# Sums of squares for the head norms: ScalarE's accumulator output in place of a VectorE reduction

## What is computed

```python
def _ln(x, w, b):
    mu = jnp.mean(x, axis=-1, keepdims=True)
    var = jnp.mean(jnp.square(x - mu), axis=-1, keepdims=True)
    return (x - mu) * jax.lax.rsqrt(var + EPS) * w + b

q = _fp8_linear_pertensor(ln_out, wq, wq_scale, q_in_scale).reshape(b, s, g, hpg, d)
q = _ln(q, qln_w, qln_b)
k = _fp8_linear_pertensor(ln_out, wk, wk_scale, k_in_scale).reshape(b, s, g, d)
k = _ln(k, kln_w, kln_b)
v = _fp8_linear_pertensor(ln_out, wv, wv_scale, v_in_scale).reshape(b, s, g, d)
core = _gqa(q, k, v).reshape(b, s, nh * d)
```

## Time and profile before

| | before |
|---|---|
| median of 3 runs | 2023.72 us (2023.13 to 2024.34) |
| profiled execution, its own time | 2026.58 us |
| its span in the trace | 2024.8 us |
| busy PE / DVE / ACT / POOL | 85% / 76% / 70% / 58% |
| granted clock of TensorE, mean | 0.977 |
| DMA | 240.88 MB, mean 119 GB/s |

### The profile page before, as it was taken

How to read it: one execution, slowest core, us unless ns; L and a number is a source line. 1 busy time by engine, 2 the same in 40 slices (tenths; PEclk the granted TensorE clock), 3 DMA queues, 4 the chain that set the end, 5 groups by cost and what they waited for, 6 DMA issues and landing times.

```text
span 2024.8 us, 48234 instructions
## 1 busy us (share of the span) xinstructions
PE 1722.7 (85%) x15776; PEld 1235.7 (61%) x15776; DVE 1531.0 (76%) x3480; ACT 1408.5 (70%) x2926; POOL 1172.4 (58%) x1045
## 2 busy tenths in 40 slices
PE   0015989999998999998999999999999768999998
PEld 0014767876776777677777767776877433444443
DVE  8996799899789979988997998899878633233232
ACT  2235889988988888898888889888999724030211
POOL 3454667776776777777777777677777602120202
PEclk9997999999999999999999999999999878999999
DMA  4100576776687677767767766776789983021100
GB/s 143 49 31 1 100 137 122 141 140 133 120 143 138 120 131 141 134 125 138 142 114 133 144 124 132 141 142 112 143 162 169 226 255 142 11 115 52 72 21 21
DMA packets 639383, 240.88 MB, mean 119 GB/s; under 512 B 612496, under 2 KB 612496, under 8 KB 638608
## 3 DMA queue, kind: packets, MB, share of 16 engines
q1 hardware_dynamic: 639120, 237.62, 57.8%
HBM read 65.57 MB, written 20.97 MB: 43 GB/s over the span
## 4 chain that ended last, share of the span: by engine, by line
issue 44%; POOL 32%; DVE 8%; ACT 6%; PE 6%; SPq 1%; DMA 1%; POOLq 1%; DVEq 0%; ACTq 0%
POOL local L976 16%; POOL head_rstd L952 7%; POOL local L959 6%; POOL local L990 3%; PE ps_pj L564 2%; ACT local L765 1%; ACT local L839 1%; DVE local L1093 1%; ACT local L842 1%; SPq L458 1%; DMA local<-local 1%; DVE local L1089 1%; DVE local L1069 1%; DVE local L1080 1%; ACT local L786 1%
## 5 line engine op out<-in xcount | busy, mean ns | idle before, releaser
L976 POOL TENSOR_TENSOR local<-local 128x512 bf16<-128x512 f32 x512 | 602.2, 1176 | 396.7 <-ACT local L842 396.7
L564 PE MATMUL ps_pj<-wide 128*128 (+2 forms) x5544 | 589.9, 256 | 10.2 <-ACT local L765 8.2
L564 PEld LDWEIGHTS ps_pj<-wide 128*128 128x128 bf16 x5544 | 471.2, 99 | 130.3 <-issue 11.5
L839 ACT ACTIVATE local<-ps_s,neg_max 128x512 f32<-128x512 f32 x512 | 375.8, 734 | 117.9 <-DVE neg_max L1191 117.0
L614 PE MATMUL ps_o<-v_hi,local 128*128 128x129 bf16 x2048 | 382.9, 224 | 71.9 <-DMA local<-local 31.5
L842 ACT ACTIVATE local<-ps_s,neg_max 128x512 bf16<-128x512 f32 x512 | 376.7, 736 | 13.6 <-DMA local<-local 13.6
L1191 DVE TENSOR_REDUCE neg_max<-ps_s 128x1 f32<-128x512 f32 x512 | 345.3, 674 | 54.0 <-PE ps_s L630 53.4
L616 PE MATMUL ps_o<-v_hi,local 128*128 128x129 bf16 x2048 | 381.9, 221 | 0.0
L615 PE MATMUL ps_o<-local 128*128 128x128 bf16 x2048 | 381.7, 220 | 0.0
L614 PEld LDWEIGHTS ps_o<-v_hi,local 128*128 128x128 bf16 x2048 | 200.9, 98 | 101.9 <-DVE local L1199 43.6
L765 ACT ACTIVATE local<-ps_pj,head_rstd 128x128 f32<-128x128 f32 x756 | 231.1, 407 | 36.9 <-POOL head_rstd L952 36.4
(11 more groups left out here) (111 smaller groups left out, 2866.9 us busy)
## 6 DMA issues: line engine op xcount, KB each, us to landing
w_raw<-w_group SPq DMA_DIRECT2D x32, 512.0 KB, 3.9
quantised_heads<-local SPq DMA_DIRECT2D x32, 512.0 KB, 3.4
wide<-quantised_heads SPq DMA_DIRECT2D x4, 4096.0 KB, 14.0
local<-local SPq DMA_TRANSPOSE x640, 3.2
local<-x SPq DMA_DIRECT2D x4, 1024.0 KB, 5.8
local<-ctx_t SPq DMA_DIRECT2D x4, 1024.0 KB, 5.0
w_raw<-w_proj SPq DMA_DIRECT2D x8, 512.0 KB, 4.5
wide<-w_proj SPq DMA_DIRECT2D x4, 1024.0 KB, 6.1
```

The lines of the kernel that those rows point to most:

```text
L564: last = mm(dst[:, at:at + n], lhs, w_at(par, part, c, cross * 512 + at, n), start=(k == 0), stop=(k == len(terms) - 1))
L839: a(p_exp[:, u % 2], ps_s[u % 2][:], ACT.Exp, bias=neg_max[:, u % 4:u % 4 + 1])
L976: tt_(pp[:, u % PP_BUFS, 1], p_exp[:, u % 2], pp[:, u % PP_BUFS, 0], ALU.subtract)\
```

## The change

ACT's one square over 384 columns becomes three over 128, one for each head, each with an accumulator output into that head's column of `sq_sum`. DVE's `head_squares` and the semaphore `red_done` go. `sq` gets two buffers and bf16 for F32; nothing reads it. The squares of tile t wait from t = 2 on for `var_done` to reach t - 1, in place of `red_done` reaching t. DVE's first instruction of a tile is now `v_rest`, and `head_variance` waits for `sq_done`.

```diff
-        sq = carve([3 * D], F32)
+        sq = carve([2, 3 * D], BF16)
...
             def squares(i, t):
                 act.wait_ge(proj_done, t + 1)
-                act.wait_ge(red_done, t)
-                a(sq[:], tile_bank(i, t)[:, 0:3 * D], ACT.Square).then_inc(sq_done, 1)
+                if not isinstance(t, int) or t >= 2:
+                    act.wait_ge(var_done, t - 1)
+                for h in range(3):
+                    last = a(sq[:, i % 2, h * D:(h + 1) * D], tile_bank(i, t)[:, h * D:(h + 1) * D], ACT.Square,
+                             accum_out=sq_sum[:, i % 2, h:h + 1])
+                last.then_inc(sq_done, 1)
...
-            def head_squares(i, t):
-
+            def head_variance(i, t):
                 dve.wait_ge(sq_done, t + 1)
-                v.tensor_reduce(sq_sum[:, i % 2, 0:3], sq[:].rearrange("p (h d) -> p h d", h=3), AX_X, ALU.add)\
-                    .then_inc(red_done, 1)
-
-            def head_variance(i, t):
-                dve.wait_ge(red_done, t + 1)
                 v.tensor_scalar(head_var[:, i % 2, 0:3], sq_sum[:, i % 2, 0:3], 1.0 / D, EPS, ALU.mult, ALU.add)\
                     .then_inc(var_done, 1)
...
             for i in range(TILES):
-                head_squares(i, i)
                 v_rest(0, i, i)
                 head_variance(i, i)
...
                     for k in tile_at(slot, VAR_LAG, first, last):
-                        head_squares(tile_place(k)[1], GROUP_TILES * g + TILES + k)
                         v_rest(*tile_place(k), GROUP_TILES * g + TILES + k)
                         head_variance(tile_place(k)[1], GROUP_TILES * g + TILES + k)
```

More of the change, by code:

```diff
@@ L241, in block_kernel @@
         vlo_done = sem("vlo_done")
-        red_done = sem("red_done")
         var_done = sem("var_done")
```

## The result

The changed kernel takes 2033.3 us (median of 5, 2032.1 to 2036.7) against 2023.3 for the kernel before in the same comparison: ratio 1.0054, 95% interval 1.0039 to 1.0068. It is slower by 10 us. I had forecast slower, but by 41 us.

A forecast was written before the change was run, and what follows sets the result against it. PE, DVE and ACT, close together and waiting for each other, bound the kernel; ACT would become fullest. +5.4 us a pass over 7.9 passes, +42.6, less 1.5 at the start, gave +41: 2065 us, range 1996 to 2140.

The forecast's parts named there:

- the first rival: Whole kernel: accumulator nearly free, a head at 0.16 to 0.25 us, so faster, about 2003 us; chance 0.28.
- I take 0.35: ScalarE's squares: each head's square with accumulator costs 0.35 us, so a tile grows by 0.68 us.
- the sum over a pass: Loop pass: ACT's load becomes 177.1 us, so a pass takes 180.9 to 187.9, middle 184.4 against 179.
- 7.9 passes: Loop with first and last pass: 252 squares at 32 a pass; +5.4 us a pass gives +42.6 us.
- 7 x 0.47 = 3.3 us a pass: PE's 7 waits for DVE in a pass: each 0.47 us shorter without the sum, about 3.3 us gained.
- The third rival: Whole kernel: DVE's gain and ACT's loss cancel, a head near 0.30 us, within 0.2% of 2024 us; chance 0.10.

The follow-up runs named there:

- the cost alone: Three ScalarE squares with accumulator outputs into a tile nobody reads, VectorE's sum and old wait kept, against the kernel before: 2072.8 us against 2026.0, ratio 1.0231.

## Why the prediction was wrong

**Right:** DVE's new wait behind v_part (20.1 us, above 7.5) and the fall of both waits for DVE (15.2 to 3.9 and 6.0 to 1.9). ACT did become the fullest engine of a pass, but only just: 166.78 us against PE's 166.30 and DVE's 148.16. Of VectorE the Trainium skill states that an operation which also writes out its accumulator is two instructions ("VectorE: DVE Perf Modes", section "Two Vector instructions with no wait between them"). For ScalarE the trace shows the same: it names the read, x756. The start gained 1.9 us, as forecast (1.5), though not through the new wait.

**The direction was luck.** I forecast a pass of the loop 5.4 us longer, and it became 0.3 longer. The changed kernel is slower because of its last pass, whose stretches I had not looked at. Of my signs, ACT's busy time went up by 11.5 us a pass where I wanted 15 or more, and PE's wait for ACT at ps_s fell from 3.2 to 2.6 where I wanted it up. That PE's waits shrink in both places was the first rival's sign.

**The first step that failed: "I take 0.35".** It measured 0.25 us a head, and so +0.38 a tile for my +0.68. I had reasoned that a sum must drain before its write starts, and put 0.29 us ahead of the write. The read follows its square after 0.16, as any next instruction would, and takes 0.09. ACT's load of a pass came out at 166.8 for my 177.1.

**The second step: the sum over a pass.** With the right 0.38 my own working gives 155.3 + 12.2 = 167.5 us of ACT, a pass between 171.3 and 177.8, and a kernel some 37 us faster: a worse forecast than the one I made. My first rival said just this, faster by 16 to 28 for a head between 0.16 and 0.25. At 0.25 it measured 10 slower. The two mistakes took opposite directions, and my too dear read kept the forecast on the right side. What the sum missed: I set the length of a pass by the load of its fullest engine plus a constant idle share. An engine with 166.8 of 180 us is at its limit in some stretches and not in others. The kernel with the cost alone shows it: ACT has 17 idle microseconds in its pass and the pass is still 5 longer.

**The third: "the loop and its first and last pass hold 252 squares of 32 a pass = 7.9 passes".** I multiplied one pass of the loop. The last pass has other neighbours: no weights for DVE, eight copies more for ACT. It gave 9.3 us, the six of the loop 1.5 together, the first 2.0. The count itself was a little high: four of the 252 squares belong to the start, so the passes hold 248, or 7.75.

**The fourth: "7 x 0.47 = 3.3 us a pass is the gain that I expect from DVE alone".** It measured 5.8 a pass (179.0 to 173.2) and 43.2 us in all. PE's own waits for DVE (6.0 us) are a part only: ACT waits 15.2 us for DVE's row maxima, and PE waits for ACT in turn. I counted the last link of the chain alone. In the kernel without the sum, in the pass 719:893, these three waits are lower (they were 15.2, 6.0 and 3.2 us):

```profile
ACT local L839 <- DVE neg_max L1189: 9.3, 9, 2.1
...
PE ps_o L613 <- DVE local L1197: 1.8, 3, 1.0
...
PE ps_s L627 <- ACT local L842: 1.3, 6, 0.4
```

The third rival, "gain at DVE and loss at ACT cancel", named what happens in a pass of the loop, but I tied it to a head of 0.30 us; it holds at 0.25. A reading of the earlier trace rows was also off, without consequence: the exponential's 0.57 us does not lie on the line of 0.82 ns a column, which would give 0.47; the line fits only the two instructions of 128 and 384 columns. That v_part stands behind the longer squares, and DVE waits 20.1 us a pass for it, was not tried by itself. So its share of the interaction of 6.5 us (10.0 against 3.5) stays open.

## What to carry to other kernels

In a pipeline whose three fullest engines are busy 87 to 93% of the time, moving work from one to another is worth what the stretches say, not the means. Cut a pass by slots, measure each stretch with and without the change, and move the work only where it pays. Who is fullest in a stretch is a first guess and no more: the stretch with DVE at 97% gained nothing from its relief. Here the same edit was worth +10 us everywhere and -24 us in 13 of 32 places. Test the cost and the relief of such a move by themselves, since each was more than 40 us and hid the other. And look at the written-out first and last passes apart, as their neighbours differ.

## What I had not expected of the hardware

- An accumulator output of ScalarE shows as an instruction of its own, which takes 0.09 us from start to start; the next ACTIVATE starts while its row still runs. Its length in the rows (mean 350 ns) is four times what it costs.
- Part of DVE's relief was given back by its own instruction. The mask over int16 (L1220, now L1216) has the same shape in both kernels, and took 883 ns before and 1165 after, 4.5 us a pass; in the kernel without a sum it took 940. Rows of a pass, before and after:

```profile
L1220 DVE TENSOR_SCALAR local<-local 128x512 int16<-128x512 int16 x16 | 14.1, 883 | 0.5
```

```profile
L1216 DVE TENSOR_SCALAR local<-local 128x512 int16<-128x512 int16 x16 | 18.6, 1165 | 0.5
```

What POOL does at that moment sets the length. A long and a short one, both before the change, each with the POOL instruction that ran when it started:

```profile
806.54 1.58 POOL L976 TENSOR_TENSOR local<-local 128x512 bf16<-128x512 f32 x1 [2.26 <-ACT local L842]
...
807.01 1.25 DVE L1220 TENSOR_SCALAR local<-local 128x512 int16<-128x512 int16 x1
...
1131.06 1.16 POOL L976 TENSOR_TENSOR local<-local 128x512 bf16<-128x512 f32 x1 [1.32 <-ACT local L842]
...
1132.02 0.35 DVE L1220 TENSOR_SCALAR local<-local 128x512 int16<-128x512 int16 x1
```

Both end 0.14 to 0.15 us after POOL's does (808.26 after 808.12, 1132.37 after 1132.22). Over the whole trace 127 masks start while a POOL instruction runs, and 125 of them end 0.15 us after it; after the change it is 125 of 126. The shortest last 0.29 us, among them the two that start beside no POOL instruction. What the change moved is the start: half of the masks began at least 0.41 us into POOL's instruction before, and half within 0.12 us of its start after, so they were held for longer. `head_variance` (L1160), over three columns, shows the same: 0.16 us as a median, up to 1.07, and all 56 long ones before the change (over 0.2 us) end 0.02 us after the POOL instruction beside them. No run took POOL's work away, so what this holding costs the whole kernel stays open.
